# Two-bank maxima, indices written into the sent rows, late values evicted by ScalarE in strips, no barriers, and an unrolled tile loop in a two-layer attention and mixture-of-experts kernel

## The reference, cut

```python
x = x + tanh(g_xattn[0]) * L0_xattn(layernorm(x), ctx, Wq, Wkv, Wo)   # 16 heads of 8
x = x + tanh(g_ffn[0])   * L0_ffn(layernorm(x), gate_w, w1, w2)       # 8 experts, top 2, gelu
x = x + tanh(g_xattn[1]) * L1_xattn(layernorm(x), ctx, ctx, ...)      # the same with biases
x = x + tanh(g_ffn[1])   * L1_ffn(layernorm(x), Wr, W1, W2, ...)      # relu, layer norm at the end
# an expert layer:
top_v, top_i = top_k(logits, 2)                    # per row, of 8 experts
comb = sum(one_hot(top_i, E) * weights(top_v)[..., None], axis=2)
out  = sum over experts e of comb[e] * (act(x @ W1[e]) @ W2[e])
```

## Time and profile before

| | |
|---|---|
| median of 3 runs | 483.57 us (480.08, 483.57, 483.91) |
| the profiled execution | 483.31 us, its span 481.5 us |
| mean granted TensorE clock | 0.901 |
| busy, share of the span | PE 392.5 us (81%), DVE 334.6 (69%), POOL 233.4 (48%), ACT 213.5 (44%) |
| chain that ended last, by engine | PE 50%, DVE 18%, POOL 11%, issue 10%, DMA 4%, ACT 3% |
| attention of layer 0 | from about 12 us to the last routing scatter at 134.7 us |
| tiles of layer 0 | 139.9 to 220 us |
| attention of layer 1 | 228 to 356.5 us |
| tiles of layer 1 | 361.3 to 446 us |
| final normalization | to 481.5 us |

### The profile page before, as it was taken

The page is one execution under the profiler, slowest core; times in us unless marked ns, Lnnn a source line. Parts: engine busy times, 40 slices in busy tenths (PEclk is TensorE's granted clock), DMA queues, the critical chain, the costliest instruction groups (busy, mean ns, idle before and its releaser), DMA issues.

```text
span 481.5 us, 17026 instructions
## 1 busy us (share of the span) xinstructions
PE 392.5 (81%) x5380; PEld 307.2 (64%) x5416; DVE 334.6 (69%) x1259; ACT 213.5 (44%) x608; POOL 233.4 (48%) x370
## 2 busy tenths in 40 slices
PE   8699999998749999999489988898849999998000
PEld 4356666665529999996146665565738999998000
DVE  4568888888665666667349899988763666666592
ACT  3445444443614444440144544454434666666022
POOL 7213356658723455453203347776751444445266
PEclk9789999999668999999669999999886999999555
DMA  6967000001111222220300001001311222221611
GB/s 188 304 183 233 3 15 25 26 25 37 52 45 48 68 68 70 66 67 26 85 14 23 25 24 37 24 26 31 88 48 39 72 65 66 66 62 49 172 46 54
DMA packets 38674, 32.08 MB, mean 67 GB/s; under 512 B 6984, under 2 KB 32245, under 8 KB 38613
## 3 DMA queue, kind: packets, MB, share of 16 engines
q1 hardware_dynamic: 34069, 21.86, 16.8%
q0 software_dynamic: 4544, 9.41, 6.1%
HBM read 20.26 MB, written 10.99 MB: 65 GB/s over the span
## 4 chain that ended last, share of the span: by engine, by line
PE 50%; DVE 18%; POOL 11%; issue 10%; DMA 4%; ACT 3%; POOLq 1%; ACTq 1%; SPq 0%; DVEq 0%
PE bank L707 45%; DVE mx L1332 7%; POOL xg_rows L584 5%; PE bank L710 5%; DVE room L1400 2%; DVE x L1317 1%; DMA o_rows<-room,ids 1%; ACT room L1190 1%; POOLq L341 1%; POOL wa L684 1%; DVE mxp L1341 1%; DMA xg_rows<-xfa,slots 1%; ACTq L1187 1%; DMA room<-xg_rows 1%; DVE stats L1300 1%
## 5 line engine op out<-in xcount | busy, mean ns | idle before, releaser
L657 POOL DMA_INDIRECT o_rows<-room,ids x78 | 77.2, 989 | 99.8 <-DVE room L1565 49.3
L707 PE MATMUL bank<-room 128*128 128x128 f32 x624 | 87.4, 285 | 2.5 <-ACT room L1190 2.0
L707 PE MATMUL bank<-wa,room 128*128 x624 | 84.3, 279 | 0.2 <-ACT room L1185 0.2
L707 PEld LDWEIGHTS bank<-room 128*128 128x128 f32 x624 | 79.3, 199 | 5.6 <-ACT room L1190 3.2
L707 PEld LDWEIGHTS bank<-wa,room 128*128 128x128 f32 x624 | 77.5, 195 | 0.8 <-issue 0.7
L584 POOL DMA_INDIRECT xg_rows<-xfa,slots x64 | 64.4, 1007 | 19.9 <-issue 19.6
L1332 DVE TENSOR_REDUCE mx<-bank 128x4 f32<-128x324 f32 x128 | 54.3, 487 | 22.8 <-PE bank L707 22.3
L1103 ACT ACTIVATE room<-bank 128x384 f32<-128x384 f32 x128 | 52.4, 496 | 26.1 <-PE bank L707 26.1
L1539 DVE COPY room<-wa 128x512 f32 x78 | 33.3, 427 | 42.9 <-issue 33.3
L1058 ACT ACTIVATE room<-bank 128x128 f32<-128x128 f32 (+1 forms) x110 | 31.1, 282 | 63.8 <-PE bank L710 63.8
L1190 ACT ACTIVATE room<-bank,b_cols 128x128 f32<-128x128 f32 x156 | 44.5, 368 | 29.4 <-PE bank L707 29.0
(11 more groups left out here) (192 smaller groups left out, 667.6 us busy)
## 6 DMA issues: line engine op xcount, KB each, us to landing
room<-xg_rows SPq DMA_DIRECT2D x78, 65.5 KB, 1.8
wa<-in_L_ffn_w SPq DMA_DIRECT2D x1, 2048.0 KB, 10.3
wb<-in_L_ffn_W SPq DMA_DIRECT2D x1, 2048.0 KB, 16.8
ob<-o_rows SPq DMA_DIRECT2D x32, 64.0 KB, 1.9
wb<-o_rows SPq DMA_DIRECT2D x6, 256.0 KB, 4.6
o_rows<-room,ids POOLq DMA_INDIRECT x78, 2.3
x<-in_x SPq DMA_DIRECT2D x4, 256.0 KB, 4.7
xg_rows<-xfa,slots POOLq DMA_INDIRECT x64
```

The lines of the kernel that those rows point to most:

```text
L657: pool.indirect_dma_start(out=o_dram[l], in_=o_sb[t.slot(UN)][:, :], in_offset=None, out_offset=bass.IndirectOffsetOnAxis(ap=ids[t.slot(UN ...
L707: return pe.matmul(out_, lhsT, rhs, start=start, stop=stop)
```

## The change

Five edits. The names and numbers of lines are those of the kernel before.

1. `maxima`: two reductions instead of four, each over two banks (648 elements for each partition instead of 324). PE writes the scores for it with the key index innermost. PE's `scores` waits for the first of two reductions instead of the second of four.
2. `choose`: the indices are written as integers straight into the row `xfa`, which grows from 131 to 137 numbers; the cast is gone, and `gap` is computed once for all batches after `route`.
3. Late values of layer 0: ScalarE evicts them, with eight activations on 32 partitions each (`value_strips`), into a v_s that DVE has set to zero at the start (128 x 4608).
4. No barriers; each engine waits for what it reads.
5. `pipeline` writes all 39 tiles out. Fewer and other unread matmuls: in layer 1's attention 2 in step 0 (4 in each of the steps 0 and 1 before), after the tiles of layer 0 42 (30 before). In step 1 ACT writes xn ahead of the query's copy.

```diff
 def pipeline(eng, n, lead, deep, step):
-    trips = (n - lead) // UN
-    for s in range(lead):
-        step(Step(s))
-    with eng.Fori(0, trips) as i:
-        for u in range(UN):
-            step(Step(lead + u, i))
-    for s in range(lead + trips * UN, n + deep):
+    for s in range(n + deep):
         step(Step(s))
...
             load_tiles(0)
-            sp.wait_ge(phase, 8)
+            for r in range(UN):
+                sp.wait_ge(s_os[0][r], 16 * len(range(r, NT, UN)))
             attention()
...
                 def warm_up(s):
-                    if s < 2:
-                        unread(bank[2][:, :], 4)
+                    if s == 0:
+                        unread(bank[2][:, :], 2)
...
                 def ranks(b, s):
-                    S["f3"].wait(pe, b, 8)
+                    S["f3"].wait(pe, b, 7)
+                    if l == 0 and late_batch(s.c - 1) is not None:
+                        pe.wait_ge(v_kept, late_batch(s.c - 1) + 1)
...
+                def value_strips(b):
+                    act.wait_ge(v_made, b + 1)
+                    for j in range(G):
+                        lanes = slice(SL * j, SL * (j + 1))
+                        for lo, hi in ((0, 1), (1, NC)):
+                            ins = act.activation(
+                                v_s[lanes, b, lo:hi, :].rearrange("p c (g j d) -> p c g j d", g=G, j=G)[:, :, :, j, :],
+                                bank[7][lanes, 288 + lo * G * HD:288 + hi * G * HD]
+                                .rearrange("p (c g d) -> p c g d", g=G, d=HD),
+                                ACT.Identity, scale=keep[lanes, lo, j * HD:j * HD + 1], bias=zero_row[lanes, 0:1])
+                    ins.then_inc(v_kept, 1)
...
+                    if live(s) and s.c != 1:
+                        normed(s)
+                    if l == 0 and late_batch(s.c - 1) is not None:
...
+                        value_strips(late_batch(s.c - 1))
                     if live(b2):
                         S["mt"].wait(act, b2)
...
             def set_up():
+                link(dve.memset(v_s[:, VE:B, :, :], 0.0))
...
-                    for g in range(G):
-                        S["sc"].wait(dve, b, g + 1)
-                        dve.tensor_reduce(mx[r][:, G * g:G * g + G],
-                                          bank[g][:, 0:W].rearrange("p (c j k) -> p j c k", c=NC, j=G),
-                                          AX.XY, ALU.max).then_inc(S["mx"].sem, 1)
+                    for g in range(0, G, 2):
+                        S["sc"].wait(dve, b, g + 2)
+                        two = banks[:, 512 * g:512 * (g + 2)].rearrange("p (i w) -> p i w", i=2)[:, :, 0:W]
+                        dve.tensor_reduce(mx[r][:, G * g:G * (g + 2)].rearrange("p (i j) -> p i j", i=2),
+                                          two.rearrange("p i (j k) -> p i j k", j=G), AX.X, ALU.max)\
+                            .then_inc(S["mx"].sem, 1)
...
                     f3.wait(dve, b, 5)
-                    dve.tensor_copy(two, topi[:, :, 0:2]).then_inc(f3.sem, 1)
...
-                        values_kept(late_batch(s.c - 1), bank[7][:, 288:])
```

More of the change, by code:

```diff
@@ L44 @@
 REGION = P + NTOK
-ROW = D + 3
+ROW = D + 1 + 8
 NT = 39
@@ L273, in build @@
         r_col = sb("r_col", [P, NT], I32)
-        bank = [ctx.enter_context(nc.psum_tensor(f"bank{i}", [P, 512], F32)) for i in range(8)]
+        banks = ctx.enter_context(nc.psum_tensor("banks", [P, 8 * 512], F32))
+        bank = [banks[:, 512 * i:512 * (i + 1)] for i in range(8)]
         xg_dram = nc.dram_tensor("xg_rows", [E * REGION, ROW], F32, kind="Internal").ap()
@@ L285, in build @@
         told = {k: sem("m_" + k) for k in
-                ("wide", "ident", "rows", "keep", "less", "consts", "tg", "wT", "w", "mask", "ones", "woT", "woS", "late", "gate1", "gate1S",
+                ("wide", "ident", "rows", "keep", "less", "consts", "tg", "wT", "w", "mask", "ones", "woT", "woS", "late", "blank", "gate1", "gate1S", "cols",
                  "k0_0a", "k0_0d") + tuple(f"{k}{g}" for k in ("ctxT", "ctxS") for g in range(3)) + tuple(
                     f"{k}{l}_{g}" for l in range(2) for k, n in (("k", 3), ("kzd", 3), ("kza", 3))
-                    for g in range(n)) + tuple(f"{k}{l}" for l in range(2) for k in ("count", "tiles", "gexp"))}
+                    for g in range(n)) + tuple(f"{k}{l}" for l in range(2) for k in ("count", "tiles", "gap", "gexp"))}
         def tell(eng, name):
@@ L1024, in step @@
                         S["oc"].wait(pe, t2.back(2))
+                        if l == 0 and t2.c == 0:
+                            pe.wait_ge(v_kept, B + 4)
                         bk, e2 = bank[5 + t2.slot(2)], expert_of(t2)
@@ L1038, in _ @@
                 tail()
+                unread(bank[2 if l == 0 else 4][:, :], 12)
+                hear(pe, f"tiles{l}")
                 if l == 0:
-                    hear(pe, "kza1_1")
-                unread(bank[4][:, :], 12)
-                end_phase(pe)
-                pe.wait_ge(phase, 4 + 8 * l)
+                    for g in range(3):
+                        hear(pe, f"kza1_{g}")
+                else:
+                    pe.wait_ge(w_copied, 2 * E)
                 pipeline(pe, NT, 8, 2, experts(l))
@@ L1104, in exps, with normed @@
                         .then_inc(S["ex"].sem, 1)
+                def normed(s):
+                    S["rs1"].wait(act, Step(s.c | 1))
+                    S["t1"].wait(act, s.back(2))
+                    r = s.slot(2)
+                    act.activation(xn[r][:, :], x[:, seq(s)], ACT.Identity, scale=rstd[:, 1, r:r + 1],
+                                   bias=rstd[:, 3, r:r + 1]).then_inc(S["xn"].sem, 1)
+                def value_strips(b):
[9 more added lines that the diff above has]
+                    ins.then_inc(v_kept, 1)
                 def copied(b, o):
@@ L1122, in step @@
                         ins.then_inc(S["qe"].sem, 1)
-                    if live(s):
-                        S["rs1"].wait(act, Step(s.c | 1))
-                        S["t1"].wait(act, s.back(2))
-                        r = s.slot(2)
-                        act.activation(xn[r][:, :], x[:, seq(s)], ACT.Identity, scale=rstd[:, 1, r:r + 1],
-                                       bias=rstd[:, 3, r:r + 1]).then_inc(S["xn"].sem, 1)
+                    if live(s) and s.c != 1:
+                        normed(s)
+                    if l == 0 and late_batch(s.c - 1) is not None:
+                        if late_batch(s.c - 1) == VE:
+                            hear(act, "keep")
+                            hear(act, "blank")
+                        value_strips(late_batch(s.c - 1))
                     if live(b2):
@@ L1164, in tail @@
                             turn(g)
-                    S["f3"].wait(act, LAST)
+                    hear(act, f"gap{l}")
                     say(act.activation(gexp[:, :], gap[:, :], ACT.Exp), f"gexp{l}")
@@ L1436, in step @@
                         read_ranks(placed(s))
+                    if l == 0 and chosen(s) and late_batch(s.c - 1) is not None:
+                        dve.wait_ge(v_kept, late_batch(s.c - 1) + 1)
                     if chosen(s):
                         read_logits(chosen(s), bank[7])
-                    if l == 0 and late_batch(s.c - 1) is not None:
-                        dve.wait_ge(v_made, late_batch(s.c - 1) + 1)
-                        if live_pair(s.back(5)):
-                            S["c2"].wait(dve, s.back(5))
-                        values_kept(late_batch(s.c - 1), bank[7][:, 288:])
                     if live(Step(s.c + 2)):
@@ L1516, in route, with gate_gaps @@
                     link(ts(r_col[:, :], t_ec[:, :], float(FC), None, ALU.mult))
+                    tell(dve, "cols")
+            def gate_gaps(l):
+                link(dve.tensor_tensor(gap[:, :], top[:, :, 1], top[:, :, 0], ALU.subtract))
+                tell(dve, f"gap{l}")
             def gate_weights(l):
```

60 lines of the change are left out of this document (25 added, 35 removed).

## The result

The changed kernel takes **512.39 us** (median of four runs, 506.75 to 515.58) against 482.98 us of the kernel before beside it: ratio 1.058, 95% interval 1.048 to 1.068. It is slower, as forecast, and takes 6 us more than the 506 us forecast. Ratios here are of the runs in the chip's faster state, which leaves out one of these four (515.58), so they aren't exactly the quotients of the medians. The profiled execution took 512.46 us.

A forecast was written before the change was run, and what follows sets the result against it. Bounds: in layer 0's attention a loop between PE, DVE and ACT, in layer 1's a full DVE, in the tiles PE. 483.3 + 23.2 + 13.6 - 3.9 - 1.6 - 2.05 - 2.9 - 3.3 - 0.4 = 506 us, range 488 to 520.

The forecast's parts named there:

- Strips, +23.2: Layer 0 attention, steps 4 to 15: ACT's strips delay PE 1.58 us in 8 steps, 2.65 in 4 with ranks.
- Clock, +13.6: Layer 0 attention: PE's new stops drop its clock to half in 8 of 12 steps, 1.7 us each.
- the clock holds, 492: Rival: strips cost as forecast, but PE's stops in layer 0 attention don't drop the clock; 492 us, chance 0.22.
- Strips are cheap, 473: Rival: eight strips on ACT take 1.0 us, only the four ranks steps wait; 473 us, chance 0.12.
- in between, 485: Rival: eight strips on ACT take 2.0 us, costing 15.7 us without clock loss; 485 us, chance 0.06.
- The point of break-even, 1.9 us: Time t for eight strips where their cost, 8 x (t-1.04) + 4 x t, passes the 14.15 us of gains.
- Tiles, -3.9 and -1.6: Writing out the tile loops saves 0.55 us for each of 7 turns in layer 1, and 1.6 in layer 0.
- Barriers, -2.05: Between layer 0's tiles and the next attention: without POOL's drain, DVE's first addition starts 2.05 us sooner.
- Unread matmuls, -2.9: Layer 1's start: six of eight unread matmuls, run at low clock ahead of ready work, go; 2.9 us saved.
- Maxima and choice, -3.3 and -0.4: Fewer reductions, no cast and a single gap save DVE time: 3.3 us in layer 1, 0.4 in layer 0.
- Start, 0: Kernel start: DVE's 4.05 us memset sticks out by 0.4 us, ACT's earlier xn gives about that back; net 0.
- 5 us sooner: Sign: layer 1's first kz matmul comes 5 us sooner after the last scatter of layer 0's tiles.

The follow-up runs named there:

- gaps_filled: Changed kernel with eight or twelve unread matmuls on PE where it waited for the strips: 524.90 us, ratio 1.0299 to the kernel before.
- strips_half: Changed kernel with four strips per batch instead of eight, each over all three chunks: 511.39 us, ratio 1.0143 to the kernel before.
- before_written_out: Kernel before with the tile loops of all engines written out and nothing else of the change: ratio 0.9928.
- before_no_barriers: Kernel before without barriers between attention, tiles and layers, and with the changed kernel's unread matmuls there: ratio 0.9927.
- ranks_later: Changed kernel with PE's ranks moved behind less_max in the four steps with strips and ranks: 525.85 us, ratio 1.039 to the kernel before.
- late_on_dve: Changed kernel with the late values back on DVE, without strips, memset and PE's wait: 492.49 us, ratio 0.9706; again 496.19 us, 0.9808.
- after_again: Changed kernel unaltered, measured once more beside the kernel before (481.6 us): 509.72 us, ratio 1.0579.

## Why the prediction was right, and where it was off

- **Strips, +23.2.** The durations were 10% too high (367 and 382 ns against 410 and 434), the pitch of 0.33 us was met, and so were the eight of them: 2.67 us against 2.62. `less_max` comes at T+5.80 (5.60 forecast), ranks at T+5.54 (5.41). PE's waits are 23.8 us. With the clock held, gaps_filled costs 21.1 us more than no strips on its own chip and 25.3 more than the kernel before in its trace. The mechanism holds, and the term to about 2 us either way.
- **Clock, +13.6.** The mechanism holds: gaps_filled has 1.00 throughout and is 13 to 17 us shorter in these steps. The size was too small. The difference of the stage, 39.7 to 42.2 us, less 21.1 to 23.8 for the stops, leaves 16 to 21 us. The count of falls came out, nine and seven of twelve where 8 were taken, though 8 was a guess. The term that was mis-sized is "at half speed it costs 1.7 us": I took the shortest stretch at the low level, 3.4 us, for each fall. A granted clock of 0.78 over 114.5 us is some 50 us at 1.2 GHz (0.22 / 0.5 x 114.5), and the forecast had 8 x 3.4 = 27; the stretch after the stop at 67.4 lasts from the window at 71 to that at 78. In the profiled execution the twelve steps are 42.2 us longer where 23.2 + 13.6 = 36.8 were forecast: 5.4 of the 6.5 us between 506.0 and 512.46. The rival "the clock holds, 492" had the stops right and fell with the windows of 0.50. The Trainium skill, TensorE: Matmul & The Clock Gate, Why this matters for your kernels, by which stops as short as these were no danger, is contradicted by the row of 71 to 72 behind a stop of 2.71 us, by that of 79 to 80 in strips_half behind one of 1.77 us, and by gaps_filled.
- **Strips are cheap, 473, and in between, 485.** Both fell: eight take 2.67 us, not 1.0 or 2.0. The point of break-even, 1.9 us, is not confirmed: strips_half has 1.72 us of strips, by the formula 8 x 0.68 + 4 x 1.72 = 12.3 us against gains of 14.15, so it should be faster, and it is 1.4% slower than before. The formula leaves the clock out, and the clock is at 0.89 there.
- **Tiles, -3.9 and -1.6.** In layer 1 -4.1 and -3.2 in the two executions of the changed kernel and -3.0 in before_written_out. In layer 0 the term is about zero: 75.37, 75.03 and 76.10 against 75.91. The step that failed there is that all time above 35 x 1.90 us comes from the loop's ends; written out, it is still there. PE's listed waits in the tiles of layer 0 were only 0.5 us in total in the kernel before (2.0 in those of layer 1), so there was next to nothing to win. In the changed kernel they are 0.2 us, so it isn't waiting for code either.
- **Barriers, -2.05.** From the last scatter to DVE's first addition: 269.85 - 262.86 = 6.99 us instead of 230.05 - 221.44 = 8.61: -1.6. The forecast took DVE's evictions as what is late next. They end at 268.9, but DVE waits another 0.6 us for the load of ob. That load was issued right behind the scatter, as forecast, but takes 3.39 us to land, and took 1.95 before; the forecast had kept its old time. Why it is slower wasn't tried.
- **Unread matmuls, -2.9.** From that addition to the first kz matmul 7.04 us instead of 11.04: -4.0. With the barriers -5.6 where 4.95 was forecast, and before_no_barriers has -5.2 alone. "5 us sooner" holds.
- **Maxima and choice, -3.3 and -0.4.** -2.8 in the changed kernel's first execution, -5.1 in its second, -3.4 alone. The maximum over two banks takes 826 ns against 2 x 487. The size is right in the traces, half of it in the timed runs.
- **Start, 0.** Step 4 comes 0.4 us sooner in one execution and 1.4 later in the other; the memset takes 3.90 us (4.05 forecast).

The gains outside the twelve steps are 13.0 us in the trace of the changed kernel, where 13.75 were forecast. That this is so close has some luck in it: the unread matmuls gave 1.1 us more, the tiles of layer 0 about 1 us less.

## What to carry to other kernels

Work moved to an engine with much idle time costs by its place in that engine's order, not by its length: eight small activations ahead of a copy that another engine waits for made this kernel 5.8% slower, and the same eight behind it left it 1.4 to 2.1% faster than before. The wait that the move needed on TensorE, ahead of ranks, belongs to its price. Where the move makes TensorE stop, price the half clock behind each stop as well as the stop, with the stretches that the profile shows and not with the shortest of them. Count small activations by their number first and by their elements second, and fill a stop that can't be avoided with matmuls only where it is.

## What the runs showed of the hardware

The half clock behind stops of up to 2.7 us cost, over the twelve steps, nearly as much as the stops themselves (13 to 21 us beside 21 to 25). The granted clock was 0.78 over the stage with twelve stops up to 2.7 us, 0.89 with twelve up to 1.9 us (ranks_later), 0.89 with four of 1.8 us and short waits (strips_half), and 1.00 with the stops filled (gaps_filled).

Chips differ about as much as these changes do. The kernel before took 483.0 and 481.6 us in two sets of runs, and 508.5 and 505.6 on two other chips. On the latter ScalarE stops where the trace names no cause on this core. These are its waits in late_on_dve, whole kernel:

```profile
ACT room L1092 <- remote: 14.5, 7, 2.5
ACT wa L1047 <- remote: 2.2, 1, 2.2
```

In the changed kernel's first trace, and in that of after_again, ScalarE has no such wait. They come at the exponentials, one every few steps. What they are wasn't tried.
